# Row numbers of a gather from TensorE, the first tile's LoRA in fp32r, and the sum awaited by halves

## The reference, cut to what matters

```python
# x: (64, 32, 512) f32; two integer ids per batch row
def _L0_cond_ref(x, condition, weights):          # weights: (16, 32, 32)
    W = weights[condition]
    return jnp.einsum('bct,bcd->bdt', x, W)

def _L1_cond_ref(x, adapter_mapping, W, b, lora_As, lora_Bs):
    base_out = jnp.einsum('bti,oi->bto', x, W) + b          # W: (512, 512)
    A = lora_As[adapter_mapping]                             # (32, 512, 16)
    Bm = lora_Bs[adapter_mapping]                            # (32, 16, 512)
    lora_h = jnp.einsum('bti,bir->btr', x, A)
    lora_out = jnp.einsum('btr,bro->bto', lora_h, Bm)
    return base_out + lora_out * SCALING                     # SCALING = 2

x = x + _L0_cond_ref(x, itok_B_0_15, L0_cond_weights)
x = x + _L1_cond_ref(x, itok_B_0_23, L1_cond_W, L1_cond_b, L1_cond_lora_As, L1_cond_lora_Bs)
```

## Time and profile before

| | us |
|---|---|
| median of 3 runs | 85.16 (85.14 to 85.26) |
| the profiled execution | 84.83 |
| its span | 83.0 |
| TensorE busy | 78.5 (94% of the span) |
| VectorE busy | 60.1 (72%) |
| ScalarE busy | 52.4 (63%) |
| GpSimd busy | 33.5 (40%) |

### The profile page before, as it was taken

One profiled execution on the slowest core, in us unless ns is written; L12 is line 12 of the kernel. 1 busy time (PEld: TensorE's weight loads), 2 busy tenths in 40 slices (PEclk: granted clock), 3 DMA queues, 4 the chain that ended last, 5 costly groups with the idle time before them and its releaser, 6 DMA issues.

```text
span 83.0 us, 2012 instructions
## 1 busy us (share of the span) xinstructions
PE 78.5 (94%) x524; PEld 71.2 (86%) x524; DVE 60.1 (72%) x158; ACT 52.4 (63%) x180; POOL 33.5 (40%) x75
## 2 busy tenths in 40 slices
PE   4999599999999999999999999999999999999970
PEld 2376498899999999999999999999999999999950
DVE  2049595877879787777878787978777777869560
ACT  1555758866666675958666666667685867665520
POOL 6108843744443517080715344352608071304300
PEclk9999999999999999999999999999999999999999
DMA  2899899998476766877668778667774626130334
GB/s 24 279 349 317 202 253 216 355 252 247 142 233 197 255 197 241 198 230 196 183 205 200 210 190 241 173 238 184 236 179 155 167 91 175 30 118 0 126 126 126
DMA packets 16141, 16.07 MB, mean 193 GB/s; under 512 B 10241, under 2 KB 10626, under 8 KB 16130
## 3 DMA queue, kind: packets, MB, share of 16 engines
q1 hardware_dynamic: 14016, 11.67, 46.9%
q0 software_dynamic: 1248, 4.06, 18.6%
q10 hardware_dynamic: 866, 0.21, 1.1%
HBM read 11.74 MB, written 4.19 MB: 192 GB/s over the span
## 4 chain that ended last, share of the span: by engine, by line
PE 85%; DMA 6%; ACTq 3%; ACT 2%; DVE 1%; issue 1%; DVEq 0%
PE z_ps L565 58%; PE z_ps L602 9%; DMA a_raw<-in_lora_a 6%; PE y_ps L617 4%; PE y_ps L615 4%; PE y_ps L613 4%; PE ht_ps L589 2%; ACTq L326 1%; PE ht_ps L652 1%; PE z_ps L597 1%; DVE y_sb L552 1%; ACT L320 1%; ACTq L316 1%; ACT a_sb L391 0%; ACTq L317 0%
## 5 line engine op out<-in xcount | busy, mean ns | idle before, releaser
L565 PE MATMUL z_ps<-wa,x_hi 128*128 128x288 f32 (+2 forms) x240 | 50.1, 301 | 0.0
L565 PEld LDWEIGHTS z_ps<-wa,x_hi 128*128 128x128 f32 x240 | 38.0, 188 | 1.8 <-issue 0.5
L565 PE MATMUL z_ps<-wa,x_lo 128*128 128x288 f32 (+2 forms) x120 | 35.3, 295 | 0.0
L565 PEld LDWEIGHTS z_ps<-wa,x_lo 128*128 128x128 f32 x120 | 22.6, 188 | 0.0
L303 POOL CAST m_hi<-m_raw 128x128 fp32r<-128x128 f32 x16 | 4.8, 301 | 35.3 <-ACT m_raw L340 35.3
L294 POOL DMA_INDIRECT b_raw<-in_lora_b,b_index_slot x16 | 16.8, 1048 | 4.4 <-POOL b_index_slot L292 4.4
L384 ACT CAST z_hi<-z_ps 128x256 fp32r<-128x256 f32 x31 | 10.1, 376 | 10.2 <-PE z_ps L602 10.1
L487 DVE TENSOR_TENSOR z_lo<-z_ps,z_hi 128x256 fp32r<-128x256 f32 x31 | 11.8, 420 | 6.3 <-ACT z_hi L384 6.3
L340 ACT COPY m_raw<-w_raw 32x32 f32 x64 | 13.8, 216 | 1.8 <-DVE w_raw L519 0.9
L446 DVE TENSOR_TENSOR x_lo<-x_raw,x_hi 128x512 fp32r<-128x512 f32 x14 | 9.7, 690 | 3.7 <-ACT x_hi L352 3.7
L467 DVE TENSOR_TENSOR b_lo<-b_raw,b_hi 128x512 fp32r<-128x512 f32 x15 | 10.4, 691 | 0.5
(11 more groups left out here) (58 smaller groups left out, 76.7 us busy)
## 6 DMA issues: line engine op xcount, KB each, us to landing
out<-y_sb SPq DMA_DIRECT2D x15, 256.0 KB, 2.4
x_raw<-in_xt SPq DMA_DIRECT2D x14, 256.0 KB, 3.2
a_raw<-in_lora_a SPq DMA_DIRECT2D x60, 32.0 KB, 2.9
first_sb<-in_first SPq DMA_DIRECT2D x2, 384.0 KB, 3.9
first_sb<-in_first SPq DMA_DIRECT2D x3, 256.0 KB, 4.8
b_raw<-in_lora_b,b_index_slot POOLq DMA_INDIRECT x16, 4.0
bias_sb<-in_bias SPq DMA_DIRECT2D x1, 256.0 KB, 4.3
a_raw<-in_lora_a ACTq DMA_DIRECT2D x4, 32.0 KB
```

The lines of the kernel that those rows point to most:

```text
L565: done = nc.tensor.matmul(target, (x_lo if lo_x else x_hi)[s][:, k, :], moving(lo_w), start=first and not lo_x and not lo_w, stop=last and ...
```

## The change

- **Row numbers.** Instead of one id for each partition, a table of 5 rows by 272 integers is loaded (ids_by_j): four rows of adapters by tile and of factors (16 where a partition belongs to batch row j), and one row of ones and of p mod 16. VectorE casts it to fp32, TensorE multiplies it out in two small fp32 matmuls inside the warm-up, ahead of its seventh matmul, into the unused bank y_last, and VectorE copies the 128x16 result into b_index. Both VectorE steps stand ahead of the first addition of the identity to W. The warm-up is one matmul of 512 columns shorter.
- **Tile 0's LoRA.** The gather of tile 0 takes 128 rows: the 64 rows of B twice. h is masked as before, then copied in fp32r into the first 64 partitions of ht_sb0 and its rest into the other 64. B is split into b_hi and b_lo as in the other tiles, by round_b(0) on ScalarE and rest_b(0) on VectorE. The LoRA is the same four fp32r matmuls as in every tile.
- **Order on ScalarE.** The copy of tile 0's A comes ahead of the first half of x of tile 1; the second half comes behind A of tile 1; round_b(0) stands between x and A of tile 2.
- **The sum by halves.** TensorE's start of tile u waits for the first half of z of tile u - 2 alone; the second is awaited at the first product of the second half.
- gather_b(3) waits for b_ready instead of lora_done.

The diff, without the declarations of semaphores:

```diff
@@ -14,7 +14,8 @@
-def lora_residual_program(nc, first, xt, ids_row, ids_of_p, w0, bias, lora_a, lora_b, out):
+def lora_residual_program(nc, first, xt, ids_row, ids_by_j, w0, bias, lora_a, lora_b, out):
@@ -31,7 +32,8 @@
-    WARM_UP = (512,) * 8 + (256,)
+    WARM_UP = (512,) * 7 + (256,)
+    INDEX_AT = 6
     NX = 3
@@ -72,8 +74,8 @@
         ids_sb = sb("ids_sb", [1, 2 * B], I32)
-        ids_p_sb = sb("ids_p_sb", [P, TILES + 1], I32)
-        r_of_p = sb("r_of_p", [P, 1], F32)
+        ids_by_j_sb = sb("ids_by_j_sb", [J + 1, TILES + 2 * P], I32)
+        ids_by_j_f = sb("ids_by_j_f", [J + 1, TILES + 2 * P], F32)
         b_index = sb("b_index", [P, TILES], U32)
...
@@ -196,6 +200,8 @@
+        index_ps = y_last[:, 0:TILES]
@@ -284,16 +290,13 @@
                     pool.wait_ge(b_gathered[s], 16 * (u // NB))
-                if u == NB:
-                    pool.wait_ge(lora_done, 2)
-                elif u > NB:
-                    pool.wait_ge(b_ready, u - NB)
-                rows = slice(0, JR if u == 0 else P)
+                if u >= NB:
+                    pool.wait_ge(b_ready, u - NB + 1)
                 pool.tensor_copy(b_index_slot[s][:, :], b_index[:, u:u + 1]).then_inc(b_index_copied, 1)
...
                 pool.indirect_dma_start(
-                    b_raw[s][rows, :], None, lora_b.rearrange("s r o -> (s r) o"),
-                    bass.IndirectOffsetOnAxis(ap=b_index_slot[s][rows, 0:1], axis=0)).then_inc(b_gathered[s], 16)
+                    b_raw[s][:, :], None, lora_b.rearrange("s r o -> (s r) o"),
+                    bass.IndirectOffsetOnAxis(ap=b_index_slot[s][:, 0:1], axis=0)).then_inc(b_gathered[s], 16)
@@ -314,7 +317,7 @@
             act.dma_start(ids_sb[:, :], ids_row).then_inc(ids_loaded, 16)
-            act.dma_start(ids_p_sb[:, :], ids_of_p).then_inc(ids_p_loaded, 16)
+            act.dma_start(ids_by_j_sb[:, :], ids_by_j).then_inc(ids_by_j_loaded, 16)
@@ -367,7 +370,7 @@
                 act.wait_ge(b_gathered[u % NB], 16 * (u // NB + 1))
-                if u >= 3:
+                if u >= 2:
                     act.wait_ge(lora_done, 2 * (u - 1))
@@ -386,14 +389,15 @@
             round_w(2)
-            round_x1(0)
             act.wait_ge(a_loaded[0], 16 * J)
...
                      a_raw[0][:, :, :, :].rearrange("p j k r -> p k j r")).then_inc(a0_ready, 1)
+            round_x1(0)
+            round_a(1)
             round_x1(1)
-            round_a(1)
             round_w(KC - 1)
             round_x(2)
+            round_b(0)
             round_a(2)
@@ -463,7 +467,7 @@
             def rest_b(u):
-                dve.wait_ge(b_hi_ready, u)
+                dve.wait_ge(b_hi_ready, u + 1)
                 nc.vector.tensor_tensor(b_lo[u % 2][:, :], b_raw[u % NB][:, :], b_hi[u % 2][:, :],
@@ -473,10 +477,16 @@
                                             own_mask0[:, :, :].rearrange("p j c -> p (j c)"),
-                                            ALU.mult).then_inc(ht_ready, 1)
+                                            ALU.mult).then_inc(ht0_step, 1)
+                    dve.wait_ge(ht0_step, 1)
+                    nc.vector.tensor_copy(ht_sb[0][0:JR, :], ht0_sb[:, :]).then_inc(ht0_step, 1)
+                    dve.wait_ge(ht0_step, 2)
+                    nc.vector.tensor_tensor(ht_sb[0][JR:P, :], ht0_sb[:, :], ht_sb[0][0:JR, :],
+                                            ALU.subtract).then_inc(ht_ready, 1)
                     return
@@ -494,27 +504,24 @@
-            def index_b():
-                dve.wait_ge(ids_p_loaded, 16)
-                nc.vector.tensor_copy(r_of_p[:, :], ids_p_sb[:, TILES:TILES + 1]).then_inc(r_ready, 1)
-                dve.wait_ge(r_ready, 1)
-                nc.vector.tensor_scalar(b_index[:, :], ids_p_sb[:, 0:TILES], float(R), r_of_p[:, 0:1],
-                                        ALU.mult, ALU.add).then_inc(b_index_ready, 1)
+            dve.wait_ge(ids_by_j_loaded, 16)
+            nc.vector.tensor_copy(ids_by_j_f[:, :], ids_by_j_sb[:, :]).then_inc(ids_by_j_ready, 1)
+            dve.wait_ge(b_index_computed, 1)
+            nc.vector.tensor_copy(b_index[:, :], index_ps).then_inc(b_index_ready, 1)
             dve.wait_ge(ident_ready, 1)
...
             add_identity(1)
-            index_b()
             rest_w(0)
...
             rest_x1(0)
+            rest_a(1)
             rest_x1(1)
-            rest_a(1)
             rest_w(3)
...
             mask_ht(0)
+            rest_b(0)
             dve.wait_ge(w0_loaded, 16)
@@ -554,7 +561,14 @@
             pe.wait_ge(zeros_ready, 1)
-            for columns in WARM_UP:
+            for n, columns in enumerate(WARM_UP):
+                if n == INDEX_AT:
+                    pe.wait_ge(ids_by_j_ready, 1)
+                    nc.tensor.matmul(index_ps[:, 1:TILES], ids_by_j_f[:, TILES:TILES + P], ids_by_j_f[:, 1:TILES],
+                                     start=True, stop=True, skip_group_check=True)
+                    nc.tensor.matmul(index_ps[:, 0:1], ids_by_j_f[:, TILES + P:], ids_by_j_f[:, 0:1],
+                                     start=True, stop=True, skip_group_check=True).then_inc(b_index_computed, 1)
                 nc.tensor.matmul(ht_ps[:, 0:columns].rearrange("p (a c) -> p a c", c=P), zeros[:, :],
@@ -575,6 +589,9 @@
                     pe.wait_ge(a_ready, 2)
+                elif k == 0 and half == 1:
+                    pe.wait_ge(z_ready, 2 * (u - 1))
                 return products(u, k, z_ps[s][:, half, 0:NW],
@@ -582,7 +599,7 @@
                 if u >= 2:
-                    pe.wait_ge(z_ready, 2 * (u - 1))
+                    pe.wait_ge(z_ready, 2 * (u - 1) - 1)
@@ -592,12 +609,7 @@
                 pe.wait_ge(ht_ready, u + 1)
-                if u == 0:
-                    pe.wait_ge(b_gathered[0], 16)
-                    nc.tensor.matmul(z_of(0, half), ht0_sb[:, :], b_raw[0][0:JR, cols(half)], start=False,
-                                     stop=True, skip_group_check=True).then_inc(lora_done, 1)
-                    return
-                pe.wait_ge(b_ready, u)
+                pe.wait_ge(b_ready, u + 1)
                 for b_part in (b_hi, b_lo):
@@ -671,6 +683,8 @@
             def last_chunk(k, half):
+                if k == 0 and half == 1:
+                    pe.wait_ge(z_ready, 2 * (LAST - 1))
                 n = (HALF + 2 * AC, HALF)[half]
@@ -716,15 +730,17 @@
-    ids_of_p = _np.repeat(adapter.reshape(TILES, J).T, C, axis=0)
-    ids_of_p[:, 0] = adapter[_np.arange(P) // R % J]
+    p = _np.arange(P)
+    rows_of_b = [_np.concatenate([R * (j_of_p == _np.arange(J).reshape(J, 1)), (p % R).reshape(1, P)])
+                 for j_of_p in (p // C, p // R % J)]
+    ids_by_j = _np.concatenate([adapter.reshape(TILES, J).T, _np.ones((1, TILES), dtype=_np.int32)])
...
         "ids_row": _np.concatenate([adapter, cond]).astype(_np.int32).reshape(1, 2 * B),
-        "ids_of_p": _np.concatenate([ids_of_p, (_np.arange(P) % R).reshape(P, 1)], axis=1).astype(_np.int32),
+        "ids_by_j": _np.concatenate([ids_by_j] + rows_of_b, axis=1).astype(_np.int32),
         "w0": w0.transpose(1, 0, 2),
```

6 lines of the change are left out of this document (4 added, 2 removed).

## The result

The changed kernel takes 86.87 us (median of the runs; 86.4 to 87.61) against 85.15 for the kernel before, run beside it on the same chip: a ratio of 1.0209, 95% interval 1.0136 to 1.0281. It is slower, by some 1.7 us. Its profiled execution took 86.40 us, the shortest of its runs, with a span of 84.3 (before: 84.83 and 83.0).

A forecast was written before the change was run, and what follows sets the result against it. Bound: TensorE, never waiting in the loop, whose start the vector path sets within 0.13 us of TensorE's own. Terms 0.31 + 1.15 - 0.34 + 0.15 = +1.27 gave 86.10 profiled, 86.4 median, range 85.7 to 87.3.

The forecast's parts named there:

- The sum to tile 2's start: Tile 2's first weight load, set by the vector path, was to move from 14.97 to 16.1 to 16.3 us.
- ScalarE's order: x_hi's first half behind the a0 copy moves w_hi 3, w_lo 3 and the mask of h back: +0.31 us.
- h in two parts: Copy, subtraction and b_lo on VectorE between mask and w0-plus-identity: +1.15 us (1.10 to 1.22).
- The gathers: Gather 0, 0.55 us earlier with 128 rows, moves beside tile 1's A and may delay it: +0.15 us.
- Rival 2: The gather takes the bandwidth in full; a1 lands 0.6 late or b_raw misses b_hi: 86.9 to 87.3 us; 12%.
- The halves: TensorE starts tile 2 on the first z_lo alone: -0.34 us; zero in the other tiles.
- TensorE's LoRA in fp32r: Tile 0's LoRA falls from 1.06 to 0.48 us, but waits for b_lo and z_lo make it +1.12.
- Row numbers: Index work in the warm-up starts VectorE's first add 1.0 us later, hidden before tile 0's h products: price 0.
- The clock: Interrupted warm-up could leave TensorE at 1.2 GHz through the 16 fp32 matmuls: +3.5, 88.7 us; 5%.
- the cover: Idle time hiding a later head: h products due at 9.38, and 0.85 us more in the LoRA wait.
- Rival 1: Head's DMAs come sooner, tile 0's A landing before 7.8: 85.0 us, 7%; partly so, no change, 5%.
- Rival 4: The LoRA time saved on TensorE counts, the vector path not being bound to this order: 0.58 less, 84.6 us; 1%.

The follow-up runs named there:

- e3: Kernel before with only ScalarE's order changed (a0 copy ahead of tile 1's first x half): 85.18 us, ratio 1.002.
- e2: Kernel before with only tile 0's LoRA changed (128-row gather, b_hi and b_lo, h in two parts): 86.51 us, ratio 1.0186.
- e5: Changed kernel without the sum by halves: 87.13 us, ratio 1.0254 to the kernel before.
- e4: Kernel before with only the wait for the sum split into halves: 84.76 us, ratio 1.0001.
- e12: e2 with the halves and VectorE's order changed (w0-plus-identity ahead of the mask, w_lo 3 behind b_lo): 85.13 us, ratio 1.0023 to the kernel before.
- e6: Changed kernel with the old row numbers and the old warm-up: 86.69 us, ratio 1.0185 to the kernel before.
- e1: Kernel before with only the row numbers by TensorE inside the warm-up, old LoRA and order: 86.05 us, ratio 1.0128.
- e7: Changed kernel with the index matmuls behind eight warm-up matmuls of 512 columns: 87.44 us, ratio 1.0277 to the kernel before.
- e10: Kernel before with only the row numbers by TensorE, index matmuls behind eight warm-up matmuls: 86.21 us, runs in two groups.

## Why the prediction was right, and where it was off

The prediction gave 86.4 with a range from 85.7 to 87.3; 86.87 was measured. Its reading of the bound holds. The 0.47 has two parts, neither of them in its sum of the path: the profiled execution took 0.30 more than the 86.10 forecast for it, with the span as forecast and the rest outside it, and the median lies 0.47 above the profiled execution where the prediction carried over 0.33. The remainder is rounding.

- **The sum to tile 2's start** was 14.97 + 1.12 + 0.15 = 16.24; measured 16.21. That it fits to 0.03 owes something to two errors that cancel (next points).
- **ScalarE's order**, forecast +0.31, gave +0.28 at the mask, of which 0.04 is the later landing of A: 0.24 for the order, as e3 also shows (0.24). The difference is w_lo 3, which took 0.69 instead of 0.75.
- **h in two parts**, the largest term, was mis-sized: +1.15 forecast, +1.29 measured, beyond the upper bound of 1.22. The copy took 0.22, near the guess of 0.20 and below the 0.28 of the two-input operations on the same shape. The failing item is b_lo behind the subtraction: it was taken to start 0.20 after it, as an independent instruction. It started 0.31 after, only when the subtraction had ended (12.10, 12.41; 12.15, 12.46 in e2). That is 0.11 of the 0.14; the waits behind mask and copy make up the rest.
- **The gathers**: +0.15 for a collision with tile 1's A, measured 0. The gather came 1.1 us earlier, not 0.55, and nothing waited. Rival 2 didn't occur. The 0.55 was short because GpSimd's copy ahead of it takes 0.19 here, 0.57 before.
- **The halves**: -0.34 forecast, -0.33 measured, and 0.33 again in e5. Alone (e4) they gave 0.18, by TensorE's path.
- **TensorE's LoRA in fp32r**: two waits of about 0.9 forecast, 0.96 and 0.89 (weight loads) measured; the four matmuls start 0.12 apart, 0.48 in all. The matmul time saved is lost in these waits, as the prediction said, and e12 shows it once more: a shorter LoRA on TensorE wins nothing while VectorE feeds it.
- **Row numbers**: table's cast at 4.22 (forecast 4.3), TensorE resumes its warm-up at 5.10 (5.2), fp32 matmuls done before 9.25, h products on the a0 copy. Price 0 in the profiled execution, and by e6, but 1.1 us in e1, where no wait for b_lo covers a late clock: the term holds only for an early rise. The landing was taken rightly: the cast that waits for the table starts at 4.22, 2.8 us after the issue at 1.39, where the old table took 4.3 us.
- **The clock**: here a step was too mild. The prediction gave 5% to a clock that stays at 1.2 GHz through all 16 matmuls, at +3.5, and said of a partial rise only that the cover would take it. All 16 slow never occurred. The partial rise did in six of nine profiled executions with the index matmuls, with the h products at 10.69 to 11.60. The mask comes 1.2 us behind them (11.41 to 12.61 in the second execution of e7, 11.33 to 12.53 in e10), so the cover ends at h products at 11.53 - 1.2 = 10.3. Beyond it the same kernel with a late rise lost 0.2 against itself with an early one (7.78 and 7.59, e5) and 1.05 (8.31 and 7.26, e7, which is the changed kernel but for the place of the index matmuls). Such executions among the four runs of the changed kernel would explain why its runs spread over 1.2 us. That is argued: no slow-clock execution of the changed kernel itself was profiled, and a late A, as in the first execution of e7, would lengthen a run as much.
- **Time outside the span**: the prediction had no term for it. It is 2.10 against 1.83, so the profiled execution is 1.57 longer where the span is 1.3 longer. It came out at 2.04 to 2.12 in all seven kernels with the new LoRA part and at 1.70 to 1.83 in all seven without it. The step goes with that part; which of its pieces brings it (the 128-row gather of tile 0, b_hi and b_lo of tile 0, h in two parts) wasn't separated and is open.

Rival 1 (the head's DMAs come sooner) failed on its number: a0 at 8.96, not before 7.8. Rival 4 (the saved LoRA counts) failed with e2.

## What to carry to other kernels

Before work is taken off the engine that bounds the loop, look at which chain sets the start of the loop; here it ran through VectorE, and 0.58 us saved on TensorE cost 1.3 on that chain. Put what a long chain hangs on (here w0 plus the identity) ahead of what has slack, but don't expect more than the engine's idle time: e12, with the halves, won 1.15 us back and still ended level. Look through the chain for steps that needn't stand in it, as ScalarE's 0.64 us ahead of the m copies. When instructions are put into a clock warm-up, time many executions and profile more than one: an edit that looks free in one profile can cost over a microsecond in half of them, as in seven of e10's twelve runs.

## What the runs showed of the hardware that was not expected

- Two fp32 matmuls with 15 columns and one, put into TensorE's warm-up, go with a late rise from 1.2 to 2.4 GHz in six of nine profiled executions (weight loads 0.43 apart instead of 0.213 until beyond 8 us), against none of nine without them; a pause of 0.63 us without them had no effect in one profile and twelve runs.
- The rise differs between two executions of one program: e5 and e7 were each profiled with an early one and a late one. e10's times fall into two groups, 84.7 to 85.8 and 86.1 to 86.8, and the profile of the upper one has the late rise.
- The granted clock in the profile's rows reads 1.00 also where the loads' distance is that of 1.2 GHz (e10 and e7, 5.6 to 8.4 us).
- On VectorE the instruction behind a subtraction that read partitions 0 to 63 and wrote 64 to 127 started only at that subtraction's end (0.31 or 0.32 after its start), though it reads none of its results, in all seven kernels with it; behind the mask, as long (0.27) but written to partitions 0 to 63, the next one started after 0.21 in the kernel before.
- The landing of tile 0's A moves between executions, of one program too, by up to 1.2 us (a0 from 8.77 to 10.01), and with it the span wherever the vector path sets it.
- 0.3 us outside the span come with the new LoRA part in seven kernels out of seven.
